# A state-space layer with routed experts: the next chunk's preparation dated over all 34 slots, picks read off the match's mark, one product on GpSimd, two yacc buffers

## The reference

```
xn  = layernorm(x)
dt  = soft_clamp(softplus(xn @ Wdt.T + bdt), 0.001, 0.1)       # per token and channel
h_n = exp(soft_clamp(dt * A[:, n])) * h_n + dt * xn * B_n      # 16 states n, a scan over the tokens
y   = sum_n h_n * C_n + Dp * xn                                # h limited to a norm of 20
scores = sigmoid(xn @ router.T); s = scores + bias             # 64 experts in 8 groups
groups = the 4 groups with the largest sum of their top 2 s; picks = top 8 of s in these groups
w   = scores[picks] / sum(scores[picks]) * 2.5
out = x + y + sum_e w_e * relu(xn @ up_e)^2 @ down_e + relu(xn @ sup)^2 @ sdown
```

## Time and profile before

| | us |
|---|---|
| median of 3 runs | 571.87 |
| lowest, highest | 571.67, 572.81 |
| the profiled execution's own time | 574.56 |
| its span in the trace | 572.8 |

### The profile page before, as it was taken

One profiled execution on the slowest core, in us unless ns is written; L12 is line 12 of the kernel. 1 busy time (PEld: TensorE's weight loads), 2 busy tenths in 40 slices (PEclk: granted clock), 3 DMA queues, 4 the chain that ended last, 5 costly groups with the idle time before them and its releaser, 6 DMA issues.

```text
span 572.8 us, 7918 instructions
## 1 busy us (share of the span) xinstructions
PE 508.6 (89%) x1666; PEld 278.0 (49%) x1666; DVE 496.0 (87%) x1158; ACT 470.4 (82%) x922; POOL 469.3 (82%) x430
## 2 busy tenths in 40 slices
PE   2158899998898988999899998999989998999996
PEld 1034445554454545565455544555445554555552
DVE  3657899899988899899998899888998899979984
ACT  2768798799886998888986998879988889988872
POOL 2389898897888979897988978889897979968762
PEclk9999999999999999999999999999999999999999
DMA  8956865887869877987678877697769877699951
GB/s 200 326 166 229 277 258 197 318 291 259 247 191 348 276 261 232 347 271 262 247 239 307 304 264 248 197 364 264 272 216 321 300 249 246 219 318 353 317 189 37
DMA packets 65649, 149.32 MB, mean 261 GB/s; under 512 B 14048, under 2 KB 31040, under 8 KB 65600
## 3 DMA queue, kind: packets, MB, share of 16 engines
q1 hardware_dynamic: 63728, 147.07, 76.3%
q10 hardware_dynamic: 1872, 1.75, 0.9%
HBM read 143.03 MB, written 5.77 MB: 260 GB/s over the span
## 4 chain that ended last, share of the span: by engine, by line
POOL 28%; issue 22%; DVE 18%; PE 14%; ACT 8%; DMA 8%; SPq 1%; POOLq 1%; DVEq 0%; ACTq 0%
POOL yacc L546 10%; DMA bc_rows<-bc_dram 7%; PE DN L1088 7%; POOL bc_rows L537 6%; DVE DC L944 4%; DVE relu L885 4%; POOL xn L444 3%; DVE g L831 3%; DVE bc_rows L897 3%; PE U L1038 2%; PE U L1039 2%; PE U L1040 2%; ACT act L715 2%; POOL rstd L438 1%; POOL rest L527 1%
## 5 line engine op out<-in xcount | busy, mean ns | idle before, releaser
L1088 PE MATMUL DN<-act,down 128*128 128x512 f32 x512 | 261.9, 593 | 1.9 <-ACT act L715 1.9
L715 ACT ACTIVATE act<-relu 128x512 f32<-128x512 f32 x272 | 169.5, 623 | 44.6 <-DVE relu L885 38.3
L885 DVE SCALAR_TENSOR_TENSOR relu<-U,gate_rows 128x512 f32<-128x512 f32 x256 | 173.6, 678 | 34.0 <-PE U L1040 17.8
L546 POOL TENSOR_TENSOR yacc<-yacc,bc_rows 128x512 f32<-128x512 f32 x120 | 154.5, 1287 | 44.9 <-DVE bc_rows L897 44.9
L1038 PE MATMUL U<-x_hi,up_hi 128*128 128x512 f32 x256 | 163.4, 638 | 23.5 <-DVE relu L885 22.5
L537 POOL TENSOR_TENSOR bc_rows<-dtx_all,bc_rows 128x512 f32<-128x512 f32 x128 | 164.4, 1285 | 20.2 <-DMA bc_rows<-bc_dram 20.2
L944 DVE TENSOR_TENSOR_SCAN DC<-DC,carry,bc_rows 128x512 f32<-128x512 f32 x96 | 122.7, 1278 | 0.0
L1088 PEld LDWEIGHTS DN<-act,down 128*128 128x128 f32 x512 | 95.3, 188 | 28.7 <-ACT act L715 6.6
L1038 PEld LDWEIGHTS U<-x_hi,up_hi 128*128 128x128 f32 x256 | 48.2, 188 | 113.7 <-DVE relu L885 70.1
L1039 PE MATMUL U<-x_lo,up_hi 128*128 128x512 f32 x256 | 101.2, 395 | 0.0
L1040 PE MATMUL U<-x_hi,up_lo 128*128 128x512 f32 x256 | 101.1, 395 | 0.0
(11 more groups left out here) (113 smaller groups left out, 501.5 us busy)
## 6 DMA issues: line engine op xcount, KB each, us to landing
bc_rows<-bc_dram SPq DMA_DIRECT2D x128, 512.0 KB, 6.0
gate_rows<-gate_dram SPq DMA_DIRECT2D x128, 512.0 KB, 4.8
xs<-in_L_attn_x SPq DMA_DIRECT2D x8, 256.0 KB, 5.6
down<-in_L_ffn_down_w SPq DMA_DIRECT2D x8, 256.0 KB, 4.9
xr<-in_L_attn_x SPq DMA_DIRECT2D x8, 256.0 KB, 5.6
rest_kept_dram<-rest SPq DMA_DIRECT2D x8, 256.0 KB, 4.3
out<-res SPq DMA_DIRECT2D x8, 256.0 KB, 4.5
dtx_all<-in_L_ffn_up_w SPq DMA_DIRECT2D x3, 512.0 KB, 5.6
```

The costliest lines, as they stand in the source:

```text
L546: g.tensor_tensor(yacc[:, :], yacc[:, :], c_rows[:, (c * N + n) % BUFS, :], ALU.add).then_inc(yacc_done, 1)
L715: a.activation(act_at(c, slot), relu[:, slot % 2, :], ACT.Square).then_inc(sq_done, 1)
L885: v.scalar_tensor_tensor(out=relu[:, slot % 2, :], in0=U[slot % 2][:, :], scalar=0.0, in1=gate_rows[:, k // 2 % SBUFS, slot % 2, :], op0=A ...
L1088: mm(DN[:, :], w, act_at(c, slot), start=slot == 0, stop=slot == SLOTS - 1).then_inc(down_done, 1)
```

## The change

A table of dates, `due(c, slot)`, tells each engine which part of whose preparation stands in a slot. The front of a preparation (dates -5 to -1) lies in slots 29 to 33 of the chunk before the one in which the rest is done:

| part | slot before | slot after |
|---|---|---|
| DVE statistics, aggregation | 0 | 29, 30 of the chunk before |
| GpSimd variance and root | 1 | 31 of the chunk before |
| GpSimd xn, four parts | 2 | two in 32, two in 33 of the chunk before |
| PE transposes xn; ACT x_hi; DVE x_lo | 4; 4; 5 | 1; 2; 3 |
| PE logits, their transposes, z | 6, 8, 10 | 4, 6, 9 |
| ACT logits, rows stored, exp, z, log | 7, 8, 9, 11, 16 | 5, 6, 7, 10, 14 |
| DVE reciprocals | 10 to 11, two and two | 8, 9, 9, 10, one each |
| GpSimd bias | 12 | 11 |
| DVE max8 by group | 13 to 15 | 11 to 14, eight each |
| DVE group sums; best groups | 16; 16 | 15 (ahead of the scan); 15 |
| DVE top 8; replaced; picks | 20; 21, 22; 22 | 20, 21; 22, 23; 24 |
| picks times scores | DVE 22 | GpSimd 24 |
| picks times roots, GpSimd | 22 | 24 |
| DVE sum of weights; GpSimd root and scaling | 23; 23 | 26; 26 |
| PE transposes cc; ACT gates out | 26; 26 | 29; 30 |
| PE out_mm; DVE result | 19; 20 | 11; 12 |

Chunk 0 prepares chunk 1 at its own dates: the front in slots 0 to 3, the rest up to date 16 four slots later than in the table, and dates 17 to 24 two to a slot in slots 21 to 24. It also holds the front of chunk 2 in slots 29 to 33. The two compares on DVE become single-source compares with the mark that `match_replace` writes. `yacc` has two buffers, and `ymul` of state 0 waits for the `out_begin` of one chunk earlier. On SP's queue the load of x moves behind row 4 and is that of the chunk after, a chunk's gates are each issued one row later, and `store_rest` and `store_result` go ahead of rows 10 and 12.

```diff
+        def due(c, slot):
+            if c == 0:
+                if slot < 21:
+                    mine = [slot - 4] if slot else [-FRONT, -4]
+                elif slot < 25:
+                    mine = [2 * slot - 25, 2 * slot - 24]
+                else:
+                    mine = [slot]
+                mine = [(1, p) for p in mine if p < SLOTS - FRONT]
+            else:
+                mine = [(c + 1, slot)] if slot < SLOTS - FRONT else []
+            if slot >= SLOTS - FRONT:
+                mine.append((c + 2, slot - SLOTS))
+            return [(pc, p) for pc, p in mine if pc < NCH]
...
                 for n in range(N):
-                    if n == 0 and not last:
-                        x_next(c)
+                    if n == 5 and c + 2 < NCH:
+                        x_next(c + 1)
                     if n == 6:
                         x_result(c - 1)
-                    if n == 11:
+                    if n == 10:
                         store_rest(c - 1)
-                    if n == 15:
+                    if n == 12:
                         store_result(c - 1)
                     rows(c, n)
-                    if n:
-                        gates_in(c, n - 1)
+                    if n > 1:
+                        gates_in(c, n - 2)
+                gates_in(c, N - 2)
                 gates_in(c, N - 1)
...
-                if slot == 22:
+                if slot == 24:
                     pool.wait_ge(picked_ready, pc + 1)
                     pool.wait_ge(roots_done, 2 * pc + 2)
                     wait(pool, ct_done, pc)
                     alone(pool)
+                    g.tensor_tensor(masked[:, :, :], picked[:, :, :], sig[:, :, :], ALU.mult).then_inc(psig_ready, 1)
...
-                    v.tensor_tensor(g1c[:, :], g1a[:, :], g1b[:, :], ALU.not_equal).then_inc(groups_ready, 1)
+                    v.tensor_scalar(g1c[:, :], g1b[:, :], TAKEN, None, ALU.is_equal).then_inc(groups_ready, 1)
...
-                    v.tensor_tensor(picked[:, :, :], picked[:, :, :], masked[:, :, :],
-                                    ALU.not_equal).then_inc(picked_ready, 1)
-                if slot == 22:
-                    dve.wait_ge(picked_ready, pc + 1)
-                    ch.then(v.tensor_tensor(masked[:, :, :], picked[:, :, :], sig[:, :, :], ALU.mult))
-                if slot == 22.5:
-                    ch.wait()
+                    v.tensor_scalar(picked[:, :, :], picked[:, :, :], TAKEN, None, ALU.is_equal).then_inc(picked_ready, 1)
+                if slot == 25.5:
+                    dve.wait_ge(psig_ready, pc + 1)
                     v.tensor_reduce(wsum[:, :], masked[:, :, :], axis=AX.X, op=ALU.add).then_inc(wsum_ready, 1)
...
                 if n == 0:
-                    wait(dve, ot_begun, c)
-                dst = c_rows[:, (c * N + n) % BUFS, :] if n else yacc[:, :]
+                    wait(dve, ot_begun, c - 1)
+                dst = c_rows[:, (c * N + n) % BUFS, :] if n else yacc[:, c % 2, :]
...
+                    if slot == 29 and not last:
+                        cc_mm(c + 1)
+                    for pc, p in due(c, slot):
+                        prep(pc, p)
...
+                    if slot == 30 and not last:
+                        gates_out(c + 1)
```

More of the change, by code:

```diff
@@ L517, in out_begin @@
                 alone(pool)
-                g.tensor_tensor(ot[:, :], rest[:, par(c)], yacc[:, :], ALU.add).then_inc(ot_begun, 1)
+                g.tensor_tensor(ot[:, :], rest[:, par(c)], yacc[:, c % 2, :], ALU.add).then_inc(ot_begun, 1)
             def out_end(c, last=False):
@@ L805, in prep @@
                     ch.then(i)
+                if slot == -4:
                     ch.wait(True)
@@ L809, in prep @@
                     i.then_inc(var_ready, 1)
-                if slot == 3 and pc == 0:
+                if slot == -2 and pc == 0:
                     dve.wait_ge(rstd_ready, 1)
@@ L840, in prep @@
                     ch.then(i)
-                if slot == 16.5:
+                if slot == 15.5:
                     op(v.memset, gtop[:, :, TOPG:], 3.0e38)
-                if slot == 17:
-                    ch.wait(True)
-                    for k in range(KB):
+                if slot in (16, 17):
+                    if slot == 16:
+                        ch.wait(True)
+                    for k in range(KB // 2) if slot == 16 else range(KB // 2, KB):
                         groups = slice(k * G, (k + 1) * G)
@@ L911, in chunk @@
             def chunk(c, first, last):
-                if not last:
-                    chains["v"] = Chain(dve, dve_prep, (c + 1) * DVE_PREP)
                 for slot in range(SLOTS):
@@ L925, in chunk @@
                         norms(c - 1)
-                    if not last:
-                        prep(c + 1, slot - 0.5)
-                    if slot == 20 and not first:
+                    for pc, p in due(c, slot)[:1]:
+                        prep(pc, p - 0.5)
+                    if slot == 12 and not first:
                         result(c - 1)
@@ L945, in chunk @@
                                              ALU.mult, ALU.add).then_inc(scan_done, 1)
-                    if not last:
-                        prep(c + 1, slot)
-                assert last or chains["v"].n == DVE_PREP, chains["v"].n
-            chains["v"] = Chain(dve, dve_prep, 0)
-            for slot in range(SLOTS):
+                    for i, (pc, p) in enumerate(due(c, slot)):
+                        if i:
+                            prep(pc, p - 0.5)
+                        prep(pc, p)
+                assert last or chains[c + 1].n == DVE_PREP, chains[c + 1].n
+            for pc in range(NCH):
+                chains[pc] = Chain(dve, dve_prep, pc * DVE_PREP)
+            for slot in range(-FRONT, SLOTS - FRONT):
                 prep(0, slot - 0.5)
@@ L1125, in chunk @@
                         down_mm(c, 0)
-                    if slot == 19 and not first:
+                    if slot == 11 and not first:
                         out_mm(c - 1)
-                    if not last:
-                        prep(c + 1, slot)
+                    if slot == 29 and not last:
+                        cc_mm(c + 1)
+                    for pc, p in due(c, slot):
+                        prep(pc, p)
             def out_mm(c):
@@ L1141, in _ @@
             pe.wait_ge(proj_ready, 2)
-            for slot in range(SLOTS):
+            for slot in range(-FRONT, SLOTS - FRONT):
                 prep(0, slot)
+            cc_mm(0)
             pe.wait_ge(dve_init, 3)
```

172 lines of the change are left out of this document (89 added, 83 removed).

## The result

The changed kernel takes 591.29 us (median of 4 runs, 590.24 to 592.11), the kernel before beside it on the same chip 572.34 (571.67 to 573.63): a ratio of 1.033 [1.031, 1.034], slower by 3.3%. The profiled execution took 590.24 us with a span of 588.5. One execution of one experiment kernel, x8_product_only, took 658.97 us in a slower state of the chip (granted clock 0.76) and is left out of that kernel's ratio.

What follows compares the result with a forecast made beforehand. No engine bounds all: VectorE's router in slots 9 to 23, PE elsewhere; after the change, GpSimd from slot 24 to slot 1. Six chunks +9.1, prologue +1.7, chunk 0 -1.5, last chunk +1.2: +10.5, so 582 us; range 557 to 594.

Steps and rivals of the forecast that it cites:

- its own mechanism: Slot 24 to slot 1: GpSimd bounds and PE waits for xn; 574 to 590 us, chance 0.50.
- gates late: Rival, slower still: the gates' store and load make slot 3 come at 26.5 instead of 24.9; 592 us, chance 0.08.
- GpSimd's list, slot 24 to xn: GpSimd's slots 24 to 33: 21.95 us of work, so xn stands 23.3 us after slot 24 began.
- The wait costs 3.2 us a chunk: Slot 24 to slot 2: relu of slot 3 at 24.9 us, against about 21.7 without PE's wait for xn.
- Slots 9 to 23: The middle piece, bounded by the router on VectorE: from 33.64 to 31.7 us.
- the +0.5 for instructions held by GpSimd: Slots 9 to 23: VectorE waits for GpSimd's SBUF access, +0.3 at the group sums and +0.2 for the two compares.
- The wait for the biased scores: Slots 9 to 23: VectorE's first max8 waits 1.15 us for GpSimd's bias add, 0.29 before: +0.85.
- Slots 3 to 8: Chunk's first piece: xn transposes leave, a reciprocal and the logits' transposes come in; from 11.41 to 11.7 us.
- Prologue: Before the chunks: GpSimd's added work after the picks makes cc ready at 34.4 instead of 32.6, +1.7 us.
- Chunk 0: First chunk: product off VectorE -1.3, xn a slot later -1.0, router work pressed together +0.8: -1.5 us.
- Last chunk: Gates stored from slot 30 instead of 26, with no wait for xn to hide it: +1.2 us.
- The spreading works: Rival, faster: GpSimd keeps its dates, xn is there at 21.7; 64.25 us a chunk, 558 us, chance 0.15.

Runs made afterwards that it cites:

- x8_product_only: The kernel before with only the product of picks and scores moved to GpSimd (slot 22), its sum in slot 23: 566.68 us, ratio 0.989 to the kernel before.
- x4_fill: The changed kernel with 12 unused PE matmuls while PE waits for xn in slot 1: 582.25 us, ratio 1.017 to the kernel before.
- x1_scores_first: The changed kernel with GpSimd's bias add ahead of the injection in slot 11: 579.36 us, ratio 1.011 to the kernel before.
- x11_front_scores_rest: The changed kernel with root and xn ahead of slot 31's injection, bias add ahead of slot 11's, x times Dp in the next chunk's slot 2: 561.38 us.
- x3_psig_dve: The changed kernel with the product of picks and scores back on VectorE in slot 24: 578.21 us, ratio 1.012 to the kernel before.
- x5_xn_act: The changed kernel with xn of chunks 1 to 7 made on ScalarE in slots 32 and 33: 578.65 us, ratio 1.009 to the kernel before.

## Why the prediction was right, and where it was not

The direction and the mechanism were right, the size was not: the forecast added 10 us to the kernel before, the change cost 19.0 (591.29 against 572.34). The measured time lies in the range of 557 to 594, but above the 574 to 590 that the text gave its own mechanism, and next to the 592 of "gates late", which did not happen. That the wide range held it, by 3 us, is luck: what the forecast left out, PE's clock, was worth 9.9. Point by point:

- **GpSimd's list, slot 24 to xn: right.** Forecast 21.95 us of work and xn 23.3 us after slot 24 began; it stood at 248.35, 23.2 after 225.15. PE's wait: 3.2 forecast, 3.16 measured. Here the text summed durations that its rows show.
- **What the late xn costs: too small.** "The wait costs 3.2 us a chunk" is where it failed. The text took PE to be as fast behind the wait as before it. It wasn't: slot 3 began 2.55 us behind xn instead of 1.6, and slots 3 to 8 took up to 1.7 longer. x4_fill gives this missing term 9.9 us. Its time, 582.25, is the forecast to a quarter of a microsecond by luck: its chunks 1 to 6 take 404.4 us where 409.2 were forecast, chunk 0 gained less than forecast, and its end is 2.2 us longer than that of the other kernels, behind the last work of PE, for a reason that no run here shows.
- **Slots 9 to 23: 31.7 forecast, 31.0 measured.** VectorE's busy time fell by 2.66 (31.99 to 29.33) and its idle time stayed, 1.65 and 1.64. Two steps failed. The compare moves from slot 22 to slot 24 and so leaves this piece; I counted only the product and the sum. It is one of the rows below, at slot 24:

```profile
296.59 0.39 DVE L899 TENSOR_SCALAR picked<-picked 128x256 f32<-128x256 f32 x1
```

  And the +0.5 for instructions held by GpSimd came out near 0.15: the group sums' median went from 0.21 to 0.36 us, while the compare's went from 0.42 to 0.37, between 0.29 (with GpSimd idle, in the prologue) and 1.08. The held instructions end when GpSimd's running one does: the group sums of chunk 3 at 279.42, 0.07 us behind an accumulation, the compare above at 296.98, 0.15 behind an injection. Both GpSimd instructions were nearly over when VectorE's began, so the holds were short. The Trainium skill ("SBUF — State Buffer", "two separate sides") says that a VectorE instruction with two inputs from SBUF, or in a two-port mode, and a GpSimd one exclude each other for the whole instruction of whichever starts first. The group sums, with two inputs, agree; whether the compare works in such a mode no run here shows. The wait for the biased scores was forecast at 1.15, measured at 1.12, and x1_scores_first shows that removing it gives all of it back.
- **Slots 3 to 8: 11.7 forecast, 11.8 at full clock.** In the kernel before, GpSimd's injections waited 18.2 us for row loads between 100 and 510 us, and some of its chunks took up to 13.2 for this piece; in the changed one these waits are 0.9 us in the whole run, and with the clock up every chunk takes 11.8 or 11.9. I had taken the short value without saying that it needs this. Which of the moves on SP's queue took these waits away was not tried by itself.
- **Prologue: +1.7, measured +1.71.** The four terms written there add up to 5.0 us, so to 34.5 and +1.9 and not to 34.4; the weights did stand at 34.51. **Chunk 0: -1.5 forecast, -0.3 measured**: its slots 3 to 8 lost 1.9, but slots 0 to 2 grew by 0.3, 9 to 23 by 0.4, and 24 to 33 by 0.9, where chunk 2's front was added, which the term left out. **Last chunk: +1.2 forecast, 0.0**: the store of the gates landed in 2.7 us there, not 6.6, and the first gate's load was waited for 0.3 us.
- **"Gates late"** did not come: all the other stores of the gates landed in 2.2 to 2.8 us too (2.3 to 8.5 in the kernel before), and no relu of chunks 1 to 6 waited for a gate. **"The spreading works"** needed GpSimd to keep its dates, and did not come; but its sum of 64.25 us a chunk is what x11_front_scores_rest reaches (64.0 to 64.8, 561.4 against its 558). The change had the gain in it, and lost it by the place of xn in one engine's order.

## What to carry to other kernels

When work is moved to an engine with idle time, sum that engine's list up to each result that another engine waits for, not over the stretch: here the root and xn, 4.6 us at the end of the list, were what was wanted first, and putting them ahead of two instructions with slack gave back 21.5 us without any work saved, about half of it the clock's. When a result is moved to a new engine, look at the last input's place in the old one: the wait follows it, and blocks what is queued behind it there. And a wait of TensorE costs more than its length when the clock falls behind it; compare the same matmul's duration on both sides of the wait.

## What the hardware showed that I had not expected

PE's clock fell to half at waits that are short: in the changed kernel PE stood 3.2 us in five of six chunks, and each time the granted clock was 0.50 for 3.4 or 6.8 us (in chunk 1, with 2.6 us of idle time, it wasn't). The length of the wait does not settle it. In chunks 0 to 6 of all kernels here the clock fell at 10 of 11 waits of 3.1 to 3.5 us, at 4 of 10 of 2.3 to 2.6 and at 2 of 6 of 2.1 to 2.2; none of the six waits of 1.5 to 1.6 us in x3_psig_dve brought a fall, but one of 1.5 us just ahead of chunk 4 of x5_xn_act did. What sets the two cases of one length apart these runs do not show. 12 unused matmuls in each wait kept the clock up and gave 9.9 us. The Trainium skill, "TensorE: Matmul & The Clock Gate", Part 1, says that the clock has these two levels and is set by how busy PE has been recently; the traces show only these two levels, and all these falls stand at idle time of PE. The same section puts the penalty of the ramp from the lower level under 1% of a typical kernel; here, where the clock fell again in five chunks, it was 9.9 of 588.5 us, 1.7%.

And a product of 256 columns is priced by its place more than by its engine: in the kernel before it took 1.3 us of the piece that VectorE bounds, and 0.7 us of GpSimd's idle time once moved there (566.68 against 572.7); where xn stood behind it, it cost 13 us (591.29 against 578.21, the clock's share included).
